# Delta stored with its high part twice and loaded by four transfers a chunk, in a selective-scan kernel on one core

## What is computed

```python
delta = softplus(dt + b_dt)                    # (B, L, D)
dA = exp(delta_t[:, :, None] * A[None])        # A = -exp(A_log), (D, 32)
dBu = (delta_t * u_t)[:, :, None] * B_t[:, None, :]
h = dA * h + dBu                               # a step of the scan over L
y_t = einsum('bdn,bn->bd', h, C_t)
```

## Time and profile before

| What | us |
|---|---|
| median of 3 runs | 958.17 |
| the 3 runs | 958.17, 995.27, 947.65 |
| the profiled execution | 962.21 |
| its span, first to last instruction | 960.1 |
| first scan begins | 66.72 |
| span by engine: PE, DVE, ACT, POOL busy | 850.7, 758.1, 503.7, 460.2 |
| PE's mean granted clock, share of full | 0.865 |

### The profile page before, as it was taken

One profiled execution on the slowest core, in us unless ns is written; L12 is line 12 of the kernel. 1 busy time (PEld: TensorE's weight loads), 2 busy tenths in 40 slices (PEclk: granted clock), 3 DMA queues, 4 the chain that ended last, 5 costly groups with the idle time before them and its releaser, 6 DMA issues.

```text
span 960.1 us, 21876 instructions
## 1 busy us (share of the span) xinstructions
PE 850.7 (89%) x7436; PEld 631.8 (66%) x7436; DVE 758.1 (79%) x773; ACT 503.7 (52%) x897; POOL 460.2 (48%) x782
## 2 busy tenths in 40 slices
PE   5568999999899898989998999997999878999985
PEld 4457665766666566667666766775766547887874
DVE  8704994998599869967986688997589937899884
ACT  4216754676557647654765466774345234445531
POOL 6404652564265446534652465573124624466344
PEclk9767995999799979985997589998589869999997
DMA  2971774577449638754964496487435332200101
GB/s 63 200 159 54 120 211 100 121 123 228 127 95 180 169 89 126 222 126 106 136 200 116 90 150 168 100 128 219 95 77 115 108 113 88 74 23 23 45 23 66
DMA packets 245313, 114.59 MB, mean 119 GB/s; under 512 B 166864, under 2 KB 238032, under 8 KB 245200
## 3 DMA queue, kind: packets, MB, share of 16 engines
q1 hardware_dynamic: 238864, 109.16, 49.7%
q10 hardware_dynamic: 6336, 3.93, 1.5%
HBM read 58.43 MB, written 54.62 MB: 118 GB/s over the span
## 4 chain that ended last, share of the span: by engine, by line
PE 43%; DVE 17%; SPq 15%; issue 10%; ACT 5%; POOL 4%; DMA 4%; DVEq 0%; ACTq 0%; POOLq 0%
DVE arena L1813 11%; PE psum L1352 8%; PE psum L1422 8%; PE psum L429 7%; PE psum L1340 7%; PE psum L1429 7%; SPq L983 4%; SPq L974 4%; SPq L966 3%; ACT arena L1562 2%; SPq L991 2%; PE psum L1281 2%; POOL arena L370 2%; SPq L998 2%; PE psum L1274 2%
## 5 line engine op out<-in xcount | busy, mean ns | idle before, releaser
L1813 DVE TENSOR_TENSOR_SCAN arena<-arena,psum 128x1024 f32<-128x1024 f32 x256 | 568.9, 2270 | 147.3 <-PE psum L1429 134.9
L1562 ACT ACTIVATE arena<-psum 128x512 f32<-128x512 f32 x512 | 280.4, 597 | 278.5 <-PE psum L1340 273.3
L1219 POOL TENSOR_TENSOR carry<-arena 128x64 f32<-128x64 f32 x252 | 109.5, 434 | 318.7 <-ACT arena L1562 146.8
L1340 PEld LDWEIGHTS psum<-delta_mov,a_sta 96*128 96x128 bf16 x2048 | 142.8, 109 | 167.3 <-issue 104.8
L1422 PE MATMUL psum<-du_mov,b_sta 96*128 96x128 bf16 x2048 | 179.6, 238 | 38.3 <-DVE arena L1813 22.8
L1340 PE MATMUL psum<-delta_mov,a_sta 96*128 96x128 bf16 x2048 | 183.0, 237 | 21.3 <-ACT arena L1562 15.8
L1422 PEld LDWEIGHTS psum<-du_mov,b_sta 96*128 96x128 bf16 x2048 | 142.1, 108 | 64.0 <-DVE arena L1813 35.8
L1352 PE MATMUL psum<-arena,c_sta 128*32 128x512 f32 x1024 | 168.5, 729 | 1.7 <-ACT y_rows L1569 1.7
L1429 PE MATMUL psum<-carry,ident 128*128 128x32 f32 x1024 | 168.2, 291 | 0.1
L1429 PEld LDWEIGHTS psum<-carry,ident 128*128 128x128 f32 x1024 | 154.5, 217 | 0.3 <-POOL carry L1217 0.3
L429 PE MATMUL psum<-delta_mov,arena 128*128 128x256 f32 (+6 forms) x544 | 117.7, 376 | 7.1 <-ACT arena L550 7.1
(11 more groups left out here) (177 smaller groups left out, 841.3 us busy)
## 6 DMA issues: line engine op xcount, KB each, us to landing
du_mov<-du_terms SPq DMA_DIRECT2D x128, 192.0 KB
du_terms<-arena SPq DMA_DIRECT2D x42, 512.0 KB, 6.7
y<-y_rows SPq DMA_DIRECT2D x32, 256.0 KB
delta_terms<-arena SPq DMA_DIRECT2D x48, 128.0 KB, 5.2
delta_mov<-delta_terms SPq DMA_DIRECT2D x128, 48.0 KB
b_sta<-b_terms SPq DMA_DIRECT2D x128, 48.0 KB
b_terms<-small SPq DMA_DIRECT2D x42, 128.0 KB, 2.1
arena<-in_L_attn_x SPq DMA_DIRECT2D x8, 512.0 KB, 3.6
```

Source lines behind the costliest of these rows:

```text
L1219: ins = pool.tensor_tensor(carry[:, g, :], seg[:, :, 0], before[:, :, TS - 1], ALU.mult)
L1340: mm = nc.tensor.matmul(psum[:, (4 + u % 2) * BANK + i * P:(4 + u % 2) * BANK + (i + 1) * P], a_sta[0:ROWS, dg * P:(dg + 1) * P], sub(delt ...
L1562: nc.scalar.activation(sub(arena, 0, P, u * 16 * TS, (TS, 16), (decay_at(k, 1), SUBS), (1, TS)), sub(psum, 0, P, (4 + u % 2) * BANK, (TC, ...
L1813: nc.vector.tensor_tensor_scan(arena[:, STATE_AT[s] + o:STATE_AT[s] + o + GD * TS], arena[:, decay_at(k, s) + o:decay_at(k, s) + o + GD * TS],
```

## The change

- Delta's scratch has four entries instead of three: high, middle, high, low (`D_ENTRIES`). The six moving terms are then entries 0, 1, 2 and entries 1, 2, 3: one DRAM pattern with outermost counts 2 and 12. `load_md` issues one transfer of 24 rows a quarter, 4 a chunk instead of 12; the bytes are the same. The stationary pieces are put in the order that fits (`A_STATION`). `store_delta` is issued 8 times a tile instead of 6.
- SP's order: `store_b` moves from kk = 0 to kk = 2; delta's high part is stored as soon as it is made, the low part after `store_y`; in kk = 2 the next tile's first `load_md` stands ahead of `store_du` and waits for delta's stores; du's high part has a semaphore of its own.
- `units_at`: kk = 3 has two units a step, steps 0 and 1 of kk = 0 too, and the steps 2 to 7 of kk = 0 have 2, 0, 2, 2, 3, 3 units for the chunk after.
- PE's B and C products (L1281) are spread over the tile's steps 0, 2, 4 and 6, a batch in each; the transpose of C stands in the last step of the tile before; the pieces that follow on ACT and POOL are moved to fit (`Exp` in piece 0, `Ln` in piece 2, the B pieces in 6, 9, 10 and 14).
- Start: delta, du and b of chunk 0 are stored first (32 of 128 positions), delta's loads start when chunk 0's are stored, the rest follows; 12 units are made ahead of chunk 0's first step, 4 in step 0.

The core of the diff:

```diff
@@ -35,7 +35,8 @@
 PARTS = 3
 MOVING_PART = (0, 1, 2, 0, 1, 0)
 STATION_PART = (0, 0, 0, 1, 1, 2)
-RUNS = ((0, 3), (3, 2), (5, 1))
+D_ENTRIES = (0, 1, 0, 2)
+A_STATION = (0, 0, 1, 1, 2, 0)
 ROWS = DQ * TERMS * B
 QROWS = TERMS * B
 DU_ROW = 2 * D
...
-        delta_terms_d = scratch("delta_terms", [LT, PARTS, B, CT, D, TC], BF16)
+        delta_terms_d = scratch("delta_terms", [LT, len(D_ENTRIES), B, CT, D, TC], BF16)
...
         AHEAD = 2
-        FIRST_UNITS = UNITS // GROUPS
+        FIRST_UNITS = 3 * UNITS // GROUPS
 
         def units_at(first, kk, step):
 
-            if first and kk == 0 and step < GROUPS - 1:
-                return [(0, (step + 1) * FIRST_UNITS + i) for i in range(FIRST_UNITS)]
-            if first and kk == 0 and step == GROUPS - 1:
-                return [(1, i) for i in range(2 * UNITS_PER_STEP)]
-            if kk == 0 and step < AHEAD:
-                return []
-            if kk == CT - 1 and step >= AHEAD:
-                edges = (0, 3, 6, 9, 12, 14, UNITS)
+            if first and kk == 0 and step < AHEAD:
+                return [(0, u) for u in range(FIRST_UNITS, UNITS)] if step == 0 else []
+            if kk == 0 and step >= AHEAD:
+                edges = (0, 2, 2, 4, 6, 9, 12)
                 return [(1, u) for u in range(edges[step - AHEAD], edges[step - AHEAD + 1])]
             at = (step - AHEAD) % STEPS * UNITS_PER_STEP
             return [(int(step >= AHEAD), at + i) for i in range(UNITS_PER_STEP)]
...
-        MD_LOADS = DQ * len(RUNS)
+        MD_LOADS = DQ
         MU_LOADS = 8
-        D_STORES = 2 * PARTS
+        D_STORES = 2 * len(D_ENTRIES)
+        D_LATER = D_STORES * (CT - 1)
+        HI_TERMS = MOVING_PART.count(0)
+        MIDLO_TERMS = TERMS - HI_TERMS
...
+                              a_parts.rearrange("p (s q n) -> p s q n", s=3, q=DQ)[:, A_STATION[s]])\
                    .then_inc(S["a_stored"], 16)
...
-            def store_delta(p, k, s, done):
+            def store_delta(p, e):
                 for h in range(2):
-                    sp_.dma_start(dram(delta_terms_d, (p * PARTS + s) * (B * CT * D * TC) + h * P * TC,
+                    sp_.dma_start(dram(delta_terms_d, (p * len(D_ENTRIES) + e) * (B * CT * D * TC) + h * P * TC,
                                        (TC, P), (D * TC, B * CT), (1, TC)),
-                                  dparts[k][s][:, h * BANK:(h + 1) * BANK].rearrange("p (c t) -> p c t", t=TC))\
-                        .then_inc(S[done], 16)
-
-            def store_du(p, part):
+                                  dparts[NEW][D_ENTRIES[e]][:, h * BANK:(h + 1) * BANK]
+                                  .rearrange("p (c t) -> p c t", t=TC)).then_inc(S["d_stored"], 16)
+
+            def store_first_delta(e, cc, done):
+                for h in range(2):
+                    sp_.dma_start(dram(delta_terms_d, e * (B * CT * D * TC) + cc * (D * TC) + h * P * TC,
+                                       (TC, P), (CT * D * TC, B), (1, TC)),
+                                  dparts[0][D_ENTRIES[e]][:, h * BANK:(h + 1) * BANK]
+                                  .rearrange("p (b c t) -> p b c t", b=B, t=TC)[:, :, cc, :]).then_inc(S[done], 16)
...
             def load_md(lt, cc):
                 k = cc % 2
                 for q in range(DQ):
-                    for row, parts in RUNS:
-                        sp_.dma_start(sub(delta_mov[k], q * QROWS + row * B, parts * B, q * TC * DG, (1, TC * DG)),
-                                      dram(delta_terms_d, lt * (PARTS * B * CT * D * TC) + (cc * D + q * DG) * TC,
-                                           (CT * D * TC, parts * B), (1, TC * DG))).then_inc(md_loaded[k], 16)
+                    sp_.dma_start(sub(delta_mov[k], q * QROWS, QROWS, q * TC * DG, (1, TC * DG)),
+                                  dram(delta_terms_d, lt * (len(D_ENTRIES) * B * CT * D * TC) + (cc * D + q * DG) * TC,
+                                       (B * CT * D * TC, 2), (CT * D * TC, 3 * B), (1, TC * DG)))\
+                        .then_inc(md_loaded[k], 16)
...
+            sp_.wait_ge(S["first_parts"], FIRST["dhi"])
+            store_first_delta(0, 0, "d0_first")
+            store_first_delta(2, 0, "d0_first")
+            sp_.wait_ge(S["first_parts"], FIRST["dmid"])
+            store_first_delta(1, 0, "d0_first")
+            sp_.wait_ge(S["first_parts"], FIRST["dlo"])
+            store_first_delta(3, 0, "d0_first")
+            for e in range(len(D_ENTRIES)):
+                store_first_delta(e, 1, "d0_stored")
+            sp_.wait_ge(S["zeros_ready"], 1)
+            sp_.wait_ge(S["d0_first"], 16 * D_STORES)
+            load_md(0, 0)
+            for cc in range(2, CT):
+                for e in range(len(D_ENTRIES)):
+                    store_first_delta(e, cc, "d0_stored")
+            sp_.wait_ge(S["du0_zeroed"], 1)
+            sp_.wait_ge(S["u0_first"], 16 * TERMS)
+            load_du(0, 0)
+            sp_.wait_ge(S["b0_first"], 16 * TERMS)
+            load_b(0, 0)
+            for s in range(TERMS):
+                if MOVING_PART[s]:
+                    sp_.dma_start(dram(du_terms_d, s * (B * L * DU_ROW) + TC * DU_ROW,
+                                       (DU_ROW, P - TC), (L * DU_ROW, B), (1, DU_ROW)),
+                                  uparts[0][MOVING_PART[s]].bitcast(BF16)[TC:P, :].rearrange("p (b n) -> p b n", b=B))\
+                       .then_inc(S["u0_stored"], 16)
+            for s in range(TERMS):
+                part = bparts[0][TC:P, STATION_PART[s] * B * P:(STATION_PART[s] + 1) * B * P]
+                sp_.dma_start(dram(b_terms_d, s * (B * L * P) + TC * P, (P, P - TC), (L * P, B), (1, P)),
+                              part.rearrange("p (b n) -> p b n", b=B)).then_inc(S["b0_stored"], 16)
             store_base(0, 0)
-            for s, made in enumerate(("dhi", "dmid", "dlo")):
-                sp_.wait_ge(S["first_parts"], FIRST[made])
-                store_delta(0, 0, s, "d0_stored")
-            sp_.wait_ge(S["zeros_ready"], 1)
-            sp_.wait_ge(S["d0_stored"], 16 * D_STORES)
-            load_md(0, 0)
-            sp_.wait_ge(S["du0_zeroed"], 1)
-            sp_.wait_ge(S["u0_stored"], 16 * TERMS)
-            load_du(0, 0)
-            sp_.wait_ge(S["b0_stored"], 16 * TERMS)
-            load_b(0, 0)
             sp_.wait_ge(S["zeros_ready"], 2)
+            sp_.wait_ge(S["d0_stored"], 16 * D_LATER)
             load_md(0, 1)
             sp_.wait_ge(S["du1_zeroed"], 1)
+            sp_.wait_ge(S["u0_stored"], 16 * TERMS)
             load_du(1, 1)
+            sp_.wait_ge(S["b0_stored"], 16 * TERMS)
             load_b(1, 1)
...
                     if late and kk == 2:
-                        for part, ready in ((0, "uhi_ready"), (2, "ulo_ready"), (1, "umid_ready")):
-                            settle(sp_)
-                            sp_.wait_ge(S[ready], p)
-                            store_du(p, part)
-                    if not (last and kk >= 2):
+                        settle(sp_)
+                        sp_.wait_ge(S["args_ready"], (c + 1) * UNITS)
+                        store_b(p, NEW, "b_stored")
+                        settle(sp_)
+                        sp_.wait_ge(S["d_stored"], 16 * D_STORES * p)
+                        load_md(p, 0)
+                    elif not (last and kk >= 2):
                         settle(sp_)
                         sp_.wait_ge(S["args_ready"], (c + 1) * UNITS)
                         load_md(lt + (kk + 2) // CT, (kk + 2) % CT)
...
                     if late and kk == 1:
                         settle(sp_)
+                        sp_.wait_ge(S["dhi_ready"], p)
+                        store_delta(p, 0)
+                        store_delta(p, 2)
+                        settle(sp_)
                         sp_.wait_ge(S["dmid_ready"], p)
-                        store_delta(p, NEW, 0, "d_stored")
-                        store_delta(p, NEW, 1, "d_stored")
+                        store_delta(p, 1)
+                    if not (first and kk == 0):
+                        store_y(c - 1)
+                    if late and kk == 1:
                         settle(sp_)
                         sp_.wait_ge(S["dlo_ready"], p)
-                        store_delta(p, NEW, 2, "d_stored")
-                    if not (first and kk == 0):
-                        store_y(c - 1)
-                    if late and kk == 0:
-                        store_b(p, NEW, "b_stored")
+                        store_delta(p, 3)
+                    if late and kk == 2:
+                        for part, ready, done in ((0, "uhi_ready", "uhi_stored"), (2, "ulo_ready", "u_stored"),
+                                                  (1, "umid_ready", "u_stored")):
+                            settle(sp_)
+                            sp_.wait_ge(S[ready], p)
+                            store_du(p, part, done)
+                            if part == 0:
+                                settle(sp_)
```

(79 more changed lines are left out.)

26 lines of the change are left out of this document (11 added, 15 removed).

## The result

The changed kernel takes 1026.8 us at the median (1014.9 to 1059.9, 4 runs), the kernel before 959.9 on the same chip (947.7 to 995.3, 4 runs): a ratio of 1.070, 95% interval 1.053 to 1.088. It is slower, and the forecast of 1016 holds. A ratio and its interval are taken from the faster runs of both kernels, a median from all runs, so the two can differ by a per cent.

A forecast was written before the change was run, and what follows sets the result against it. Bound now: DVE's scans idling behind PE; after the change, two DMA engines' queue of 97 us a tile. Tiles 1 to 6 gain 58 us, start and tile 0 lose 4: 962.2 plus 54 gives 1016, range 955 to 1085.

The forecast's parts named there:

- Two engines: Delta's new load, outermost count 2 in DRAM, runs on 2 DMA engines: share near 0.12, 8.3 us a chunk.
- The budget: Queue of those two DMA engines per tile, all transfers summed: 100.0 us, taken as 97, for tiles 1 to 6.
- Rival 3: Two engines, and pauses pull the clock down too, as in chunk 8 (0.70 after 2.6 us): 1080 us; chance 0.12.
- near 18 to 20: Sign of being right: chunks of kk = 0 and 1 near 18 to 20 us, kk = 2 and 3 well above 20.
- Start and tile 0: First scan near 66 us as before, tile 0 about 101: together 4 us less (bounds 12 less, 6 more).
- SP is not late now, so nothing: SP's DMA issues: eight fewer a chunk save SP 3 us, but bring no gain in time.
- tile 7 and what follows: Tile 7 asks 73 us of the queue, no change; the last 193 us don't use what is changed.
- rival 1: Delta's load is spread as before or its packets leave the queue free: tiles 76 to 79 us, 887 in all; chance 0.14.
- 0 to 1 us: PE's new waits for z's and C's copies hold its queue 0 to 1 us a tile, around the loop's end.
- Two units a step: In kk = 3, two units instead of three: chunk 23's 21.7 back to about 19, 3 to 5 us a tile.

## Why the prediction was right, and where it was off

- **Two engines.** Right: share 0.13 where near 0.12 was forecast, 52 to 54 GB/s for some 45, 7.8 to 9.1 us a chunk for 8.3. The Trainium skill's rule ("DMA: Bandwidth & Descriptors", section "Why a DMA increments its semaphore by 16 and not by 1") gives 2 for the changed pattern and 12 with the counts exchanged; the traces agree, with two packets in flight and 2.1 engines for the first, and for the second up to 12 or 13 in flight and 0.54 x 16 = 8.6 engines over a window with both its ends. The section also has the lowest-numbered engines taken by all such transfers. No row of before showed it; y's stores in the changed kernel's packets agree, since half of each comes late beside a delta load.
- **The budget.** 97 us a tile, 582 for tiles 1 to 6; measured 580.5. Good to 0.3%, but partly by luck (the changed kernel's second profile has 574.2). Taken as a pure queue it failed: y spread out should have given 12 us a tile by it (three quarters of 16.3; the expectation says 13), and gave 3 to 4. With y spread there is still no packet in flight for only 5.2 us of a tile's 92.4, so the queue had hardly shortened; why is open. The waits were where they were forecast: kk = 2 and 3 at 22.4 and 30.4 us on average over tiles 1 to 5 (17.4 and 24.8 before), kk = 0 and 1 at 25.8 and 19.2. The 25.8 is above the forecast "near 18 to 20", and it is what before has too (25.4): the clock was left out. Rival 3's pause of 2.6 us before chunk 8 is chunk 12's; before chunk 8 the trace has 2.17.
- **Start and tile 0**, the term that was mis-sized: "4 us less", measured 12.5 more, outside its bounds of 12 less and 6 more. The steps that failed are "SP is not late now, so nothing" and the du load that went uncounted. Eight fewer issues save SP nothing when 16 stores behind the load take 18.9 us to issue, so du's load is issued at 60.7 and PE stands for b and delta:

```profile
52.50 1.01 PE L1385 MATMUL psum<-delta_mov,a_sta 96*128 96x128 bf16 x8 [8.68 <-DMA delta_mov<-delta_terms]
...
69.01 1.01 PE L1475 MATMUL psum<-du_mov,b_sta 96*128 96x128 bf16 x8 [8.95 <-DMA b_sta<-b_terms]
...
86.42 1.03 PE L1385 MATMUL psum<-delta_mov,a_sta 96*128 96x128 bf16 x8 [8.46 <-DMA delta_mov<-delta_terms]
```

  The loads were issued at 38.9, before the forecast 40 to 42, and PE had them at 52.5, within 51 to 53. The third wait, for chunk 1's delta inside tile 0, is about as long as tile 0's growth (8.2 of the 12.5).

  These 16.5 us of error were partly hidden: tiles 1 to 6 came out 1.5 under the forecast, and tile 7 and what follows, for which no change was forecast, 5.4 shorter. So the span grew by 64.0 where 54 was forecast, and the last 5.4 of the agreement are luck.
- **The price of rival 1** (887 with the load spread) was wrong by 66 to 71 us, the worst figure of the prediction, though it was given only 0.14. Two of its steps failed. It took the new order at nothing ("0 to 1 us" for new waits): with du's high part stored ahead of the delta load the time is 27 us lower. And it took kk = 0 and 3 as 18 to 19 us each beside 3 for the loop's end: kk = 3 still takes 23.5 with that store moved, and kk = 0 takes 26.8, with a granted clock of 0.62 or 0.63 in four of tiles 1 to 6, after pauses of PE of 1.5 to 3.9 us where before has at most 2.8. Had the load been spread, as rival 1 has it, the forecast would have been "faster by 8%" and the result "no change".
- **Two units a step** was sized at 3 to 5 us a tile, and some 24 us in all is what the run without it lacks: about right, though within overlapping intervals, and only once the queue was free. Start and tile 0 with 12 outermost are 18.3 us shorter than before (152.0 against 170.3), as rival 1 had it ("some 18").
- **Rival 3** (clock pulled down as well) is partly true: the granted clock is 0.81 in tiles 1 to 6 and 0.87 before. The loss that comes with it lies inside the forecast, not on top. How much of it the clock makes no run parts.

## What to carry to other kernels

When several transfers are merged into one with more dimensions, read the outermost count of both patterns: with 2 outermost the transfer ran on 2 of 16 engines, with the same counts exchanged on 12, and some 70 us lay between them. Add up time per engine, not the mean share of all: the mean fell while two engines were full. When stores are reordered, follow each one to the buffer it frees and to the engine that waits to overwrite it.

## What was not expected of the hardware

- SP's own issue slows down when stores stand behind a load: the 16 stores behind the first load took 18.9 us to issue, with the load on 12 engines still 14.2, and the 16 ahead of it 9.3 in both.
- After a pause of some 4 us PE's granted clock can stay at half for a whole chunk, although PE is busy in nearly all of it: 28.3 of 28.8 us at 0.50, in the second of the windows above. It doesn't always: the chunk at 0.62 and the one at 0.86 began after much the same pause, 3.58 and 3.80 us of PE. Nor does it need such a pause: after one of 1.15 us a chunk ran at 0.50 for 32.5 us, with PE busy for 32.0 of them. What decides stays open; the dear case costs 6 to 13 us a chunk (28 to 32.5 against 19 to 22).
- A transfer on four engines whose first two are busy lands by halves: y's store took mostly 8 to 12 us beside a delta load and 4 to 5 without one, with half of its packets landed after 4.4 us at most.
